# First cross attention: the score statistics and the weighted sums of different heads in one stream, six heads apart

## The reference

```python
scores = qk / math.sqrt(dk)                    # (16, 256, 4096)
mean_sim = scores.mean(axis=(-2, -1))
max_sim = scores.max(axis=-1).mean(axis=-1)
probs = jax.nn.softmax(scores, axis=-1)
entropy_proxy = jnp.var(probs, axis=-1, ddof=1).mean(axis=-1)
feats = jnp.stack([mean_sim, max_sim, entropy_proxy], axis=-1)
hidden = jax.nn.gelu(_linear(feats, w1, b1), approximate=False)
hidden = jax.nn.gelu(_linear(hidden, w2, b2), approximate=False)
log_t = jnp.clip(_linear(hidden, w3, b3), LOG_T_MIN, LOG_T_MAX)
t = jnp.exp(log_t)[..., None]
attn = jax.nn.softmax(qk / (2.0 * t), axis=-1)
out = jnp.einsum('bhqk,bhkd->bhqd', attn, V)
```

## Time and profile before

| | us |
|---|---|
| median of 3 runs | 1384.77 |
| all three | 1386.34, 1379.67, 1384.77 |
| the profiled execution's own time | 1379.86 |
| its span, first to last instruction | 1378.1 |

### The profile page before, as it was taken

The page is one execution under the profiler, slowest core; times in us unless marked ns, Lnnn a source line. Parts: engine busy times, 40 slices in busy tenths (PEclk is TensorE's granted clock), DMA queues, the critical chain, the costliest instruction groups (busy, mean ns, idle before and its releaser), DMA issues. The chain is left out here.

```text
span 1378.1 us, 25688 instructions
## 1 busy us (share of the span) xinstructions
PE 1121.5 (81%) x8423; PEld 688.5 (50%) x8423; DVE 821.5 (60%) x1508; ACT 895.6 (65%) x1208; POOL 630.7 (46%) x293
## 2 busy tenths in 40 slices
PE   7677877857999859979987788888888888857798
PEld 3334443433444436668872444454454544434687
DVE  6788888871010175552235788888878788925312
ACT  3699999977989724533322788888888888625110
POOL 2277778760000005000002899999999999900000
PEclk9999999987999978989995899999999999968899
DMA  7874545537555061014457999999999999524140
GB/s 250 258 219 117 130 112 133 128 92 151 111 110 107 0 223 50 1 39 152 152 214 245 325 324 316 320 321 334 315 320 324 328 331 313 179 64 175 47 137 8
DMA packets 97048, 257.51 MB, mean 187 GB/s; under 512 B 11193, under 2 KB 41305, under 8 KB 85466
## 3 DMA queue, kind: packets, MB, share of 16 engines
q1 hardware_dynamic: 96992, 256.79, 59.5%
HBM read 165.31 MB, written 91.92 MB: 187 GB/s over the span
## 5 line engine op out<-in xcount | busy, mean ns | idle before, releaser
L1920 POOL TENSOR_TENSOR xb_row<-xb_row,w_mask 128x1024 f32<-128x1024 f32 x128 | 419.2, 3288 | 240.7 <-DVE xb_row L1950 239.1
L1950 DVE TENSOR_TENSOR xb_row<-xb_cont_ps,xb_row 128x1024 f32<-128x1024 f32 x128 | 156.7, 1224 | 81.0 <-PE xb_cont_ps L1750 71.9
L1750 PE MATMUL xb_rel_ps<-xb_kk,xb_qq 32*128 32x512 f32 x496 | 146.9, 670 | 35.2 <-ACT xb_out L1868 33.7
L554 DVE TENSOR_REDUCE xa_stats<-xa_b_ps 128x1 f32<-128x1024 f32 x128 | 155.6, 1219 | 33.3 <-PE xa_b_ps L470 32.6
L1961 DVE CUSTOM_DVE_ANT_0 xb_row<-xb_row,xb_minus 128x1024 f32<-128x1024 f32 x128 | 171.6, 1341 | 0.0
L1873 ACT ACTIVATE xb_row<-xb_row,xb_ntop 128x2048 f32<-128x2048 f32 x64 | 128.3, 2005 | 51.8 <-DVE xb_ntop L1967 51.8
L1750 PE MATMUL xb_cont_ps<-xb_kk,xb_qq 32*128 32x512 f32 x528 | 157.1, 672 | 2.8 <-DVE xb_row L1950 1.7
L864 ACT ACTIVATE xa_probs<-xa_psT,xa_t_now 128x1024 f32<-128x1024 f32 x128 | 141.2, 1114 | 20.3 <-PE xa_psT L823 20.1
L522 ACT ACTIVATE xa_exps<-xa_b_ps,xa_stats 128x1024 f32<-128x1024 f32 x128 | 141.2, 1108 | 12.7 <-DVE xa_stats L554 12.5
L1868 ACT COPY xb_out<-xb_rel_ps 128x1024 f32<-128x1024 f32 x124 | 124.7, 1006 | 38.0 <-PE xb_rel_ps L1750 26.6
L1787 PE MATMUL xb_turn_ps<-_ident,xb_row 128*128 128x128 f32 x1024 | 140.6, 281 | 8.3 <-ACT xb_turned L1879 7.4
(11 more groups left out here) (364 smaller groups left out, 1821.0 us busy)
## 6 DMA issues: line engine op xcount, KB each, us to landing
xb_row<-rel_scores SPq DMA_DIRECT2D x128, 512.0 KB, 6.3
rel_scores<-xb_out SPq DMA_DIRECT2D x32, 1024.5 KB, 5.6
rel_scores<-xb_out SPq DMA_DIRECT2D x32, 1024.0 KB, 5.5
b_e_w<-in_L_ffn_e_w SPq DMA_DIRECT2D x32, 513.0 KB, 3.5
w_w<-in_L_ffn_w SPq DMA_DIRECT2D x24, 512.0 KB, 4.9
xa_k<-first_parts SPq DMA_DIRECT2D x24, 384.0 KB, 5.1
value_rows<-xa_values SPq DMA_DIRECT2D x16, 544.0 KB, 6.1
xb_kk<-key_blocks SPq DMA_DIRECT2D x17, 512.0 KB, 8.1
```

What stands on the lines that cost most here:

```text
L554: nc.vector.tensor_reduce(stats[:, c % 2, 0, u:u + 1], ps[:, slot % 4], AX, ALU.min).then_inc(s["min_ready"], 1)
L1750: mm = nc.tensor.matmul(out[:, k * BANK:(k + 1) * BANK], qq[rows, b, kind, t * P:(t + 1) * P], kk[rows, b, half], start=True, stop=True)
L1920: nc.gpsimd.tensor_tensor(row[:, held(c), at:at + SUB], row[:, held(c), at:at + SUB], mask[:, t, half * HALF + at:half * HALF + at + SUB], ...
L1950: nc.vector.tensor_tensor(row[:, held(c), at:at + SUB], cont_ps[:], row[:, held(c), at:at + SUB], ALU.add).then_inc(s["cont_out"], 1)
```

## The change

The first pass, the temperature and the second pass become one block, which is written out without loops as 22 steps. Step n makes first-pass head n (while n is under 16) and second-pass head n - 6 (from step 6 on); within a step the eight units of both alternate on each engine. The parts:

- PSUM: one ring of three slots of 1024 is shared by the units of both passes and by the temperature's small matmuls; one bank is for the products and the gathered sums, one for the sums. Exponentials of the second pass have two buffers for four, keys of the second pass two buffers of their own (`keys2`) for four, and so have its values (`vhead`).
- The squares of heads 0 to 5 are divided as before. Of heads 6 to 15, which share their steps, ScalarE squares units 2 and 4, GpSimd 0, 1, 3, 5 and 7, and VectorE unit 6 with one instruction that multiplies and sums.
- The temperature is worked out for four heads at a time, in steps 4 and 5, 8 and 9, 12 and 13, 16 and 17, in pieces between the units.
- In TensorE's order a unit of second-pass scores now stands behind the weighing of the group two before it.
- Several buffers of the first block are freed at its end.

The core of the diff (a line "..." marks what is left out):

```diff
+        LAG = 6
+        ALONE, SHARED = ((0, 2, 3, 5, 6), (1, 4, 7)), ((2, 4), (0, 1, 3, 5, 7))
+        VECTOR_SQUARE = 6
+        SLOTS = 3
+        GROUP = 4
+        STEPS = H + LAG
+        squares_of = lambda h: SHARED if h >= LAG else ALONE
...
+        def group_at(step, first):
+            g = (step - GROUP - first) // GROUP
+            return g if (step - first) % GROUP == 0 and 0 <= g < H // GROUP else None
...
-            ps = f.ps(inner, "b_ps", [P, 4, QUARTER])
+            ps = f.ps(inner, "b_ps", [P, SLOTS, QUARTER])
+            bank = f.ps(inner, "bank", [P, BANK])
+            sums = f.ps(inner, "sums", [P, BANK])
...
+                def load_second(p):
+                    b = p % 2
...
+                    if p >= 2:
+                        sp.wait_ge(s["probs_used"], NG * (p - 1))
+                    load_first_keys(f, sp, keys2[0:ROWS, b], p, kb_loaded[b])
...
+                for step in range(STEPS):
+                    if 2 <= step < H:
+                        sp.wait_ge(s["scored"], NU * (step - 1))
+                        load_first_keys(f, sp, k96[0:ROWS, step % 2], step, k_loaded[step % 2])
...
+                    if 2 <= step < H + 2:
+                        store(step - 2)
+                    if second(step) is not None:
+                        load_second(second(step))
+                    if group_at(step, 1) is not None:
+                        turn_maxima(group_at(step, 1))
...
+                    for u in range(NU):                       # TensorE
+                        if u == 4 and group_at(step, 1) is not None:
+                            hidden2(group_at(step, 1))
+                        if step < H:
+                            scores(step, u)
+                        if p is not None and u >= 2:
+                            weigh(p, u - 2)
+                        elif p is not None and p > 0:
+                            weigh(p - 1, NG + u - 2)
+                        if u % 2 == 1 and step < H:
+                            product(step, u // 2)
+                        if u == 4 and 0 <= step - LAG - 1 < H:
+                            bring_together(step - LAG - 1)
+                        if p is not None:
+                            scores2(p, u)
+                        if u == 5 and group_at(step, 0) is not None:
+                            maxima(group_at(step, 0))
+                        if u == 2 and group_at(step, 1) is not None:
+                            hidden1(group_at(step, 1))
+                        if u == 5 and group_at(step, 1) is not None:
+                            log_t(group_at(step, 1))
...
+                    for u in range(NU):                       # ScalarE
+                        if step < H:
+                            exponential(step, u)
+                        if p is not None:
+                            probabilities(p, u)
+                        if u == 2 and group_at(step, 1) is not None:
+                            hidden1(group_at(step, 1))
+                            if step < H and (step, u) in act_index:
+                                square(step, u)
+                            hidden2(group_at(step, 1))
+                        elif u == 3 and group_at(step, 1) is not None:
+                            pass
+                        elif (step, u - 1) in act_index:
+                            square(step, u - 1)
...
+                def vector_square(h):
+                    u = VECTOR_SQUARE
+                    dve.wait_ge(s["exp_done"], NU * h + u + 1)
...
+                    nc.vector.tensor_tensor_reduce(out=vector_squares[:], in0=exps[:, u % 4], in1=exps[:, u % 4], scale=1.0,
+                                                   scalar=0.0, op0=ALU.mult, op1=ALU.add,
+                                                   accum_out=stats[:, h % 2, 2, u:u + 1]).then_inc(s["vector_squared"], 1)
...
+                    for u in range(NU):                       # VectorE
+                        if step < H:
+                            minimum(step, u)
+                        if u == 0 and 1 <= step <= H:
+                            product_out(step - 1, NU // 2 - 1)
+                        if u % 2 == 0 and u > 0 and step < H:
+                            product_out(step, u // 2 - 1)
+                        if u == 1 and 0 <= before < H:
+                            take_sums(before)
+                        if u == 5 and 0 <= before < H:
+                            normalize(before)
...
+                        if u == 0 and LAG < step <= H:
+                            vector_square(step - 1)
+                        if u == 3 and 1 <= step <= H:
+                            unfold(step - 1)
+                            keep(step - 1)
+                        if u == 4 and group_at(step, 0) is not None:
+                            maxima_of(group_at(step, 0))
+                        if u == 6 and group_at(step, 0) is not None:
+                            split_maxima(group_at(step, 0))
+                        if u == 7 and group_at(step, 0) is not None:
+                            energies(group_at(step, 0))
+                        if u == 0 and group_at(step, 1) is not None:
+                            features(group_at(step, 1))
+                        if u == 6 and group_at(step, 1) is not None:
+                            clip(group_at(step, 1))
+                        if u == 0 and group_at(step, 2) is not None:
+                            scale(group_at(step, 2))
...
+                def unfold(h):
+                    dve.wait_ge(s["pool_folded"], pool_upto(h))
...
+                        nc.vector.tensor_reduce(stats[:, h % 2, 2, 0:1], folded[:, h % 2, 0], AX, ALU.add)
+                        nc.vector.tensor_reduce(stats[:, h % 2, 2, 1:NU:2], folded[:, h % 2, 1:len(SHARED[1])], AX, ALU.add
+                                                ).then_inc(s["unfolded"], 1)
```

More of the change, by code:

```diff
@@ new lines, in product, with scores2 @@
+                    mm.then_inc(s["bank_in"], 1)
+                def scores2(p, g):
+                    take_slot("second", p, g)
+                    for c in range(GC):
+                        at = (g * GC + c) * P
+                        mm = nc.tensor.matmul(slot_of("second", p, g)[:, c * S:(c + 1) * S],
+                                              keys2[0:MAXROWS, p % 2, at:at + P], q96[0:MAXROWS, p, :],
+                                              start=True, stop=True)
+                    mm.then_inc(s["scoredT"], 1)
@@ new lines, in weigh @@
+                def weigh(p, g):
+                    pe.wait_ge(s["probs_ready"], NG * p + g + 1)
+                    if g == 0 and p > 0:
+                        pe.wait_ge(s["sums_sb"], p)
+                    for c in range(GC):
+                        mm = nc.tensor.matmul(sums[c * QUAD:c * QUAD + DV, 0:S], vhead[:, p % 2, g * GC + c, :],
+                                              probs[:, g % 2, c, :], start=(g == 0), stop=(g == NG - 1))
+                    mm.then_inc(s["probs_used"], 1)
@@ new lines, in bring_together, with maxima @@
+                def bring_together(p):
+                    take_bank("both", p)
+                    pe.wait_ge(s["sums_sb"], p + 1)
+                    for t in range(NT):
+                        mm = nc.tensor.matmul(bank[:, t * QUAD:t * QUAD + DV], sumsT[:, p % 2, t * P:(t + 1) * P], gather[:],
+                                              start=True, stop=True)
+                    mm.then_inc(s["bank_in"], 1)
+                def maxima(g):
+                    take_slot("maxima", g, 0)
+                    pe.wait_ge(s["m_T"], g + 1)
+                    nc.tensor.transpose(slot_of("maxima", g, 0)[0:GROUP * NT, 0:P],
+                                        mneg[:, GROUP * NT * g:GROUP * NT * (g + 1)], f.ident[:]).then_inc(s["m_T_mm"], 1)
@@ L641, in _ @@
-                with pool.Fori(0, NB) as it:
-                    for c in range(HPB):
-                        for u in POOL_SQUARES:
-                            square(it, c, u)
-        both_passes.close()
-        k_more = f.sb(ctx, "k_more", [P, DEEP_KEYS - 2, S2], BF16)
-        vhead = f.sb(ctx, "vhead", [P, DEEP_KEYS, NCH, DV])
-        gather = f.sb(ctx, "gather", [P, DV])
-        g_loaded, more_ones = f.sem("g_loaded"), f.sem("more_ones")
-        def keys_of(b):
-            return k96[:, b] if b < 2 else k_more[:, b - 2]
@@ new lines, in square @@
+                        out = rest[:, 0:width] if k < FOLDS - 1 else folded[:, h % 2, squares_of(h)[1].index(u)]
+                        nc.gpsimd.tensor_tensor(out, rest[:, 0:width], rest[:, width:2 * width], ALU.add
+                                                ).then_inc(s["pool_product"], 1)
+                    pool.wait_ge(s["pool_product"], done + FOLDS + 1)
+                    pool.sem_inc(s["pool_folded"], 1)
+                for h in range(H):
+                    for u in squares_of(h)[1]:
+                        square(h, u)
```

737 lines of the change are left out of this document (336 added, 401 removed).

## The result

The changed kernel takes **1441.2 us** (median of four runs, 1441.0 to 1444.1) beside 1385.1 for the kernel before: a ratio of 1.0426, 95% interval 1.0406 to 1.0446. The forecast of 1350 us and its range are missed, and the sign with them.

What follows compares the result with a forecast made beforehand. ScalarE was taken to limit both passes, with TensorE beside it in the second. Terms -31 - 19.6 + 17.5 + 2.4 - 2 = -32.7 us against 1379.86 gave 1347, forecast as 1350 us; eight-in-ten range 1324 to 1377.

Steps and rivals of the forecast that it cites:

- The shared step: Steps 6 to 15: laid out at 21.2 us, taken as 22.0, bounds 20.5 and 24.5; ten steps give -31 us.
- rival 2: Tight coupling passes each wait on: 24.5 to 25 us a shared step, 1375 to 1380 us in all; chance 0.13.
- Heads 0 to 5 alone: First-pass heads before sharing: same ScalarE work, loop border gone, three slots for four; -2 us, bounds -8 and +6.
- hand work to each other lose more than either: Shared step: two engines each needing 21.2 us lose more together, so 22.0 us was taken.
- rival 1: Loose coupling, units interleave almost without waits: 20.5 us a shared step, groups at 10, about 1328 us; chance 0.17.
- The groups: Temperature work in four groups of four heads, with table loads, Gelu and short VectorE pieces: +17.5 us, bounds 8 and 28.
- VectorE's square: One square per shared step on VectorE, taken at 1.3 us; bounds 1.22 and 2.81.
- the two ways that the forecast gave for the port: Shared SBUF port: GpSimd coming second waits out VectorE's square, or a square coming second waits out GpSimd's multiply.
- The 0.95 us a step for GpSimd: Shared step: contention from one VectorE square lengthens GpSimd's work from 20.2 to 21.2 us.
- rival 3: All GpSimd work stretched 1.40 by VectorE: 28.4 us a shared step, 1414 us in all; chance 0.06.
- the gap of 19.6 us: ScalarE's gap between the two passes, from last square to 319.47 us, goes: -19.6 us.
- the last six heads: Second-pass heads alone at the end: 10.1 to 10.2 us a head against 9.78; +2.4 us, bounds 0 and +6.

Runs made afterwards that it cites:

- e1: Changed kernel with VectorE emptying the product bank at once, before the next unit's minimum, and normalizing moved from unit 5 to 4: 1383.6 us, ratio 0.9997.
- e7: e1 with VectorE's square back on ScalarE (3 squares there, 5 on GpSimd): 1373.4 us, ratio 0.9931.
- e9: e1 with GpSimd's multiply and folds cut to 16 columns, its units' sums of squares not computed: 1358.8 us, ratio 0.9826.
- e8: Changed kernel with GpSimd's multiply and folds cut to 16 columns, its units' sums of squares not computed: 1424.6 us, ratio 1.0301.
- e11: e7 with most short VectorE group pieces left out (differences, energies and features not computed): 1362.6 us, ratio 0.9851.
- e13: e7 with the maxima's split made inside PSUM, and differences, energies and features not computed: 1354.5 us, ratio 0.9789.

## Why the prediction was wrong, point by point

- **The shared step, "I laid one steady step out", "The period comes out at 21.2 us": this step failed.** The layout had the ring of three slots in it, but not TensorE's wait for the one `bank`. The text named "one bank for products and gather" only in rival 2 and priced that at 1375 to 1380. Had the wait been laid out, copy behind the next minimum and next product behind the copy, the prediction's own prices give it: a key product 1.82 us, 0.6 to a finished unit, its minimum 1.22, the bias add 0.74, in all 4.38 us a pair of units (measured 4.39) and 17.6 us a head alone, more than the 14.5 before. Measured in place of 22.0: 20.8 at first, then 26 to 27 in ordinary shared steps. e1 shows the late emptying, with the clock that fell behind it, at 57.6 us of the 91 missed, 42 of them in the shared steps.
- **Heads 0 to 5 alone, "-2, bounds -8 and +6".** The same missing wait: 17.7 us against 14.5. With the bank free it was 13.9, so the sign of -2 was right there.
- **With that wait gone, three engines at about 20 us do interleave.** 20.3 to 20.8 us is better than the 22.0 taken; "hand work to each other lose more than either" was too dark by some 15 us over ten steps, and rival 1's 20.5 right. ScalarE has 19.65 of 20 us there in e7.
- **The groups, +17.5 us with bounds 8 and 28: this term failed.** In e1 the second and third cost about 21 and 16 us, the first about 16 (22.5 + 21.0 - 2 x 13.9), and the last 9.7 by the copies of the sums: 62 us. With GpSimd nearly empty (e9) they come to 41, so some 20 are the hold and what it brings with it, and the 17.5 was short by 24 more even without a hold. Counted were 22 pieces of 0.22 us, from a stretch in which GpSimd was idle; not counted were the hold, what stands behind it, and the fallen clock. The work was put where VectorE has the minima in its queue, and a late minimum stops ScalarE and then TensorE. Groups 44 us over forecast, shared steps 15 under, and about 6 in the first two heads make e1's 34 us over 1350. These 6 were put at nothing: 3.2 are the constants in front of the bank's emptying (first distance 19.0 us against 15.8), and 2.9 stand in the first head (keep at 79.25 us against 76.34), where VectorE has the bias of the first key product only at 60.69 us and TensorE waits 4.66 us for the bank; that part was not tried.
- **VectorE's square, 1.3 us and hidden.** It took 1.76. In ordinary steps it was hidden with the bank free, beside groups it was not: 10 us in all (e1 to e7). Of the two ways that the forecast gave for the port, both came: the square waits out GpSimd, and the next GpSimd instruction waits out the square. The 0.95 us a step for GpSimd was near (0.8 us a square), though most of it falls on folds. It bound nothing (e8), and the stretch of all of GpSimd's work that rival 3 needs did not come.
- **Right:** the gap of 19.6 us goes; of the last six heads those without group work take 10.0 to 10.2 us; ScalarE's squares (50) and GpSimd's multiplies (68) number as said. The three marks of being wrong, a shared step over 23.5 us, GpSimd idle over 2 us in it, groups over 7 each, were all met.
- **The chances.** Slower had 0.07, and 0.06 of that hung on GpSimd. The one text that named an order of waits, rival 2, listed the bank among several couplings at 0.13 and did not work out its period, which could be read from the diff and the prices; no rival let it make the kernel slower than before.

## What to carry to other kernels

When a change takes a buffer from a ring and gives its users one bank, write down for that bank who fills it, who empties it and **what stands in the emptier's queue in front of it**. If that is work on the filler's next output, the two engines run in turn, however low their loads. Price short pieces that are moved beside a busy engine by rows taken beside that engine, not from the quiet stretch they come from, and put their delay through to the engine that waits last.

## What was not expected of the hardware

- A VectorE piece of 0.2 us took up to 1.8 us, ending with the GpSimd instruction under way; the pieces of the same split, with one operand in PSUM, took 0.28 us each beside the same GpSimd. It goes both ways: a GpSimd multiply of 1.89 us took 2.65 under a VectorE square that began 0.32 us before it.
- Idle time of TensorE had a tail: behind a late exponential the granted clock was 0.57 in one window (e11), and 0.87 over a whole step after waits of 0.35 and 0.81 us (e13), and a product took 3.78 us each time, where at the 2.4 GHz level a key product (e11) takes 1.98 and a value product (e13) 2.05. In e13 that product alone is 1.7 of the step's 5.9 us of excess.
